# Attention stage of a fused transformer kernel: a unit's products in a new order, and the normalisation on GpSimd

## Chip and metric
One NeuronCore of one Trainium2 chip runs the program. The metric is the device time in microseconds (us) of one execution.

## Reference
Six sublayers, each fed by a layer norm, act on x of shape (8, 512, 128): expert FFN, RWKV attention, expert FFN, top-1 MoE, causal attention, top-1 MoE. The change touches the fifth:

```
x = x + 0.5 * _L1_ffn_ref(_layernorm(x))          # the stage before
# _L1_attn_ref(_layernorm(x)): 16 heads of d_k = 8, 512 tokens
qkv = einsum('bsm,qhkm->qbhsk', x, w_qkv); Q, K, V = qkv
scores = where(causal, einsum('bhsk,bhtk->bhst', Q, K) / sqrt(d_k), -inf)
attn = einsum('bhst,bhtk->bhsk', softmax(scores), V)
x = x + einsum('bsd,md->bsm', attn_cat, w_o)
x = x + 0.5 * _L1_ffn_ref(_layernorm(x))          # the stage after
```

## The kernel before
It is written engine by engine. Every engine runs its own program in order: TensorE (PE, matmuls), VectorE (DVE), ScalarE (ACT), GpSimd (POOL) and SyncE (SP, which only issues DMAs). Semaphores tie them together; a wait that is not yet met holds back all that stands behind it on its engine. x lies in SBUF throughout.

Attention works on 8 sequences b, each in NG = 4 units g of four heads: unit u = 4b + g, 32 units. Each head has 32 rows of the array (its high and low fp16 parts side by side), so that the score products of the four heads use the four row groups. A unit's key scores (keys down, queries across, only the causal part) are KT = 12 tiles t: tiles 0 to 3 (heads 0 to 3) hold 512 columns, 4 to 7 hold 384, 8 to 11 hold 256 + 128. by_key computes tile t into PSUM bank 4 + t % 2 and first waits until ACT's exps has emptied that bank, that is for the exp of tile t - 2. exps(u, g, t) (L938) writes the probabilities, POOL's mask (L620) zeroes the part above each diagonal, and weighted_values (L2036) multiplies by V in four column groups in fp32, for j = 0 to 3 (keys j*128 on), for the unit before. ACT copies that result (values, L950), PE transposes it (transpose_values, L2043), DVE divides by the sums (normalise, L1497, L1501).

The maximum that an exp subtracts enters through an extra row of the query stack. So two units ahead, by_query (L2019) computes the scores again with queries down, in QT = 6 groups n of two heads each, in banks 0 to 3; products of a bf16 identity and a mask (L2023) add the causal mask, 128 columns each; DVE's maxima (L1490) reduces. Then max_rows (L1995) transposes the maxima of a whole unit, ACT copies them (max_copy, L945), and SP loads them into the query stack (L458). by_key waits for that DMA (s_mmax) at t = 0.

Q, K and V of the next sequence are projected one each at fixed places of units g = 0 and 1 (q_proj, k_proj, v_proj; L1590 to L1592), each through PSUM bank 7, copied by ACT (q_high L925, k_high L931, v_copy L955), completed by DVE (q_low L1475, k_low L1479), and regrouped by head by SP's DMAs (stack, L451 for Q, L453 for K). transpose_out, out_proj (L2049 and L1590 to L1592), out_high, out_low and add finish the sequence before. x of a later sequence is normalised for the next stage by prep_bn, prep_aggr, prep_rstd, prep_norm (L1037), prep_transpose (L1580).

SP's program of the stage, after the start:

```
for u in range(UNITS - 1):
    max_rows(u + 1)                  # waits s_mTc, then the DMA that s_mmax counts
    if u % NG == 0 and u // NG < NB - 1:
        for g in range(NG):
            stack(u // NG + 1, g)    # wait s_mqlo, DMA Q; wait s_mklo, DMA K
```

PE's order in a unit: before tile t, the weighted values at t = 1, 3, 5, 5; tile t; with every even t a query group with its masks; max_rows after t = MAX_AT[g] = (2, 4, 2, 4); q_proj at t = 6 and k_proj at t = 10 of g = 0; v_proj at t = 8 of g = 1; transposes and output projections at t = 6, 8, 10 of g = 2 and 3. On ACT, k_high stands behind exp 11 of g = 0; on DVE, k_low stands behind the maxima n = 0 of g = 1. The loop over sequences is Fori over pairs for b = 1 to 4, the others are written out.

Of the kernel before, what the change touches and what calls it, by code (L numbers as in the profile page):

```python
# [14 lines left out]
P = 128  # L15
# [60 lines left out]
def build(nc, x, ffn_router, ffn_w, lin, col, bias, con, half, big, out):  # L76
    with ExitStack() as ctx:
# [130 lines left out]
        neg_max = [carve(HG * SUB) for _ in range(2)]  # L208
        max_row = carve(P, F16)
# [177 lines left out]
        s_p1, s_p1used = sem("scores_by_query_in_psum"), sem("scores_by_query_used")  # L387
# [89 lines left out]
        def _(pool):  # L477
# [9 lines left out]

            def clear_bias():
                pool.wait_ge(s_wlo, 3 * E)
                pool.memset(bias_raw, 0.0).then_inc(s_bz, 1)  # L490
# [48 lines left out]
            def moe(ph):  # L539
# [3 lines left out]
                def norm(bx):  # L543
                    n = n0 + SUB * bx
                    pool.wait_ge(s_rstd, n + SUB)
                    pool.wait_ge(s_xT, n)
                    for q in range(SUB):
                        ins = pool.tensor_scalar(x_norm[:, q * P:(q + 1) * P], sub(x_tok, SUB * (bx % NB) + q), ln_neg[:, q:q + 1],
                                                 ln_rstd[:, q:q + 1], ALU.add, ALU.mult)
                    ins.then_inc(s_xn, SUB)  # L550

# [17 lines left out]
                norm(2)  # L569
                for b in range(NB):  # L570
                    if b:
                        add(b - 1)
                    if b + 3 < last:
                        prep_rstd(n0 + SUB * (b + 3))
                        norm(b + 3)
# [34 lines left out]
            def attention(ph, start, rest):  # L610
# [32 lines left out]
        def _(act):  # L643
# [266 lines left out]
            def attention(ph, start, rest):  # L910
# [105 lines left out]
        def _(dve):  # L1016
# [453 lines left out]
            def attention(ph, start, rest):  # L1470
# [10 lines left out]
                def maxima(u, g, n):  # L1481

                    if n == 0 and not (isinstance(u, int) and u < 2):
                        dve.wait_ge(s_mTp, u - 1)
                    dve.wait_ge(s_p1, QT * u + n + 1)
                    r, pieces = query_tile(n)
# [36 lines left out]
                def body(b, odd, first, prep, more):  # L1523
# [3 lines left out]
                    for g in range(NG):  # L1527
                        u = NG * b + g
                        for n in range(QT):
                            if more or g < NG - 2:  # L1530
                                maxima(u + 2, (g + 2) % NG, n)
                            if n == 0 and g == 1 and more:
                                k_low(b + 1)
                            if n == 4 and g == 0 and more:
                                q_low(b + 1)
                            if n == 4 and g == 2 and not first:
                                out_low(b - 1)
                            if n == 0 and g == 3 and not first:
                                add(b - 1)
                            if n == 4 and not (first and g == 0):  # L1540
                                normalise(u - 1, b - (g == 0), (g - 1) % NG, odd ^ (g == 0))
                            if n == 2 and g == 1 and prep:
                                prep_bn(nx, SUB * bx)
                            if n == 3 and g == 1 and prep:
                                prep_aggr(nx)
                            if n in (1, 2) and g == 2 and prep:
                                prep_norm(nx, SUB * bx, range(2 * n - 2, 2 * n))
# [27 lines left out]
        def _(pe):  # L1575
# [394 lines left out]
            def attention(ph, start, rest):  # L1970
# [21 lines left out]
                def max_rows(u, g):  # L1992

                    pe.wait_ge(s_p1used, QT * (u + 1) + 2)
# [15 lines left out]
                def by_query(u, b, g, n, odd):  # L2010
                    first, pieces = query_tile(n)
# [4 lines left out]
                    for m, (i, at) in enumerate(pieces):  # L2016
                        for x in range(2):
                            rows = head(first + x)
                            pe.matmul(bank(2 * (n % 2) + x, at, at + (i + 1) * P), q_stack[odd][g][rows, i * P:(i + 1) * P], k_stack[odd][g][rows, 0:(i + 1) * P],  # L2019
                                      start=m == 0, stop=False, skip_group_check=True)  # L2020
                    for m, (i, at) in enumerate(pieces):
                        for x in range(2):
                            ins = pe.matmul(bank(2 * (n % 2) + x, at + i * P, at + (i + 1) * P), ident_b, keys_after,  # L2023
                                            start=False, stop=True, skip_group_check=True)
                    ins.then_inc(s_p1, 1)
# [44 lines left out]
                for u in range(2):  # L2070
                    for n in range(QT):
                        by_query(u, 0, u, n, 0)
                        keep_warm(1, 6)
# [154 lines left out]
```

## Time and profile before

| | us |
|---|---|
| median of 3 runs | 1806.04 |
| lowest, highest | 1795.75, 1809.79 |
| profiled execution, its own time | 1796.81 |
| its span, first to last instruction | 1794.7 |
| mean granted TensorE clock, share of full | 0.98 |

The profile records one execution. Its times are microseconds from the start of the span, and the views below are rows of it: engine busy times, groups of instructions by line, and timelines in which neighbouring instructions of one line are merged (x8 is eight of them, and the duration runs from the first's start to the last's end). A matmul's duration holds its latency, so back-to-back starts tell its cost. The bracket at the end of a row is idle time of that engine before it and what the profile takes to have ended it.

### The profile page before, as it was taken

What the parts mean: (1) busy time and instruction counts of PE and PEld (TensorE: products, weight loads), DVE (VectorE), ACT (ScalarE), POOL (GpSimd) and SP (SyncE); (2) the same over time, 40 slices, a digit from 0 to 9 for tenths busy, and PEclk for the clock granted to TensorE, in tenths of its full rate; (3) what the DMA queues carried; (4) which work ended last, traced back from release to release, by engine and by line L of the source; (5) the groups of instructions that cost most, each with busy time, mean ns of one, the idle gap of its engine ahead of it and who ended that gap; (6) DMA issues with size and microseconds to landing.
All of it is one profiled execution on the core that took longest, in us unless ns stands there. A gap on an engine that the chain in (4) does not pass through costs nothing. (4 is left out here: it accounts for less than half of the span.)

```text
span 1794.7 us, 45173 instructions
## 1 busy us (share of the span) xinstructions
PE 1691.7 (94%) x15966; PEld 1000.2 (56%) x15966; DVE 1226.7 (68%) x2848; ACT 1017.1 (57%) x1956; POOL 876.7 (49%) x722
## 2 busy tenths in 40 slices
PE   7899999999998999979999999999999998999988
PEld 4566666666665666646666666666644343434334
DVE  5865666666667888746665665666678786888566
ACT  5655555555555566545555555566533775777633
POOL 2665765665541435556755655765443222232232
PEclk9999999999999999999999999999999998999889
DMA  4200000000000000000000000000001110111000
GB/s 144 85 20 1 0 0 0 0 0 1 2 1 2 2 0 0 2 1 1 2 1 0 0 0 0 0 1 1 2 1 25 28 37 15 43 28 25 2 13 35
DMA packets 14617, 23.41 MB, mean 13 GB/s; under 512 B 2570, under 2 KB 10890, under 8 KB 14356
## 3 DMA queue, kind: packets, MB, share of 16 engines
q1 hardware_dynamic: 14484, 21.62, 4.2%
q8 instruction: 85, 1.39, 0.3%
q14 instruction: 48, 0.39, 0.1%
HBM read 11.00 MB, written 2.10 MB: 7 GB/s over the span
## 5 line engine op out<-in xcount | busy, mean ns | idle before, releaser
L506 POOL TENSOR_TENSOR scratch<-scratch 128x512 f16<-128x512 f32 x384 | 445.5, 1160 | 416.6 <-ACT scratch L667 416.3
L667 ACT ACTIVATE scratch<-scratch 128x512 f16<-128x512 f32 x512 | 322.4, 630 | 440.7 <-DVE scratch L1110 440.6
L1110 DVE SCALAR_TENSOR_TENSOR scratch<-psum,scratch 128x512 f32<-128x512 f32 x512 | 352.9, 690 | 313.8 <-ACT scratch L662 180.1
L1628 PE MATMUL psum<-ffn_down_hi,scratch 128*128 128x128 f16 x2048 | 369.3, 219 | 2.5 <-POOL scratch L506 2.1
L1630 PE MATMUL psum<-ffn_down_hi,scratch 128*128 128x128 f16 x2048 | 369.2, 219 | 0.0
L1629 PE MATMUL psum<-ffn_down_lo,scratch 128*128 128x128 f16 x2048 | 369.2, 219 | 0.0
L662 ACT ACTIVATE scratch<-psum 128x512 f32<-128x512 f32 x512 | 296.7, 580 | 0.0
L1490 DVE TENSOR_REDUCE scratch<-psum 128x2 f32<-128x1024 f32 (+3 forms) x256 | 202.4, 822 | 56.7 <-PE psum L2023 53.5
L1628 PEld LDWEIGHTS psum<-ffn_down_hi,scratch 128*128 128x128 f16 x2048 | 200.3, 98 | 60.4 <-POOL scratch L506 3.1
L1629 PEld LDWEIGHTS psum<-ffn_down_lo,scratch 128*128 128x128 f16 x2048 | 200.4, 98 | 56.1
L1590 PE MATMUL psum<-x_hi,ffn_up_hi 128*128 (+1 forms) x512 | 195.7, 382 | 7.8 <-DVE scratch L1110 7.6
L1630 PEld LDWEIGHTS psum<-ffn_down_hi,scratch 128*128 128x128 f16 x2048 | 200.4, 98 | 0.0
L1590 PE MATMUL psum<-x_hi,ffn_gate_hi 128*128 (+1 forms) x512 | 194.7, 380 | 3.6 <-ACT scratch L662 2.7
L1591 PE MATMUL psum<-x_lo,ffn_up_hi 128*128 (+1 forms) x512 | 195.1, 381 | 0.0
L1592 PE MATMUL psum<-x_hi,ffn_up_lo 128*128 (+1 forms) x512 | 195.0, 381 | 0.0
L1591 PE MATMUL psum<-x_lo,ffn_gate_hi 128*128 (+1 forms) x512 | 194.8, 380 | 0.0
L1592 PE MATMUL psum<-x_hi,ffn_gate_lo 128*128 (+1 forms) x512 | 194.7, 380 | 0.0
L499 POOL TENSOR_TENSOR scratch<-e_const,scratch 128x16 f32<-128x16 f32 x56 | 163.4, 2917 | 0.0
L480 POOL TENSOR_TENSOR ln_rstd<-ln_var,neg_half 128x4 f32<-128x4 f32 x48 | 48.5, 1010 | 210.8 <-DVE ln_var L1030 210.8
L1125 DVE SCALAR_TENSOR_TENSOR x_tok<-psum,scratch,x_tok 128x128 f32 (+1 forms) x512 | 143.2, 343 | 5.3 <-DVE scratch L1100 2.9
L938 ACT ACTIVATE scratch<-psum 128x384 f32<-128x384 f32 x256 | 116.3, 490 | 43.0 <-PE psum L2006 41.7
L1117 DVE TENSOR_TENSOR scratch<-scratch 128x512 f16<-128x512 f32 x128 | 88.8, 694 | 52.6 <-ACT scratch L667 50.1
(225 smaller groups left out, 2861.6 us busy)
## 6 DMA issues: line engine op xcount, KB each, us to landing
raw<-in_ffn_w_dram SPq DMA_DIRECT2D x8, 768.0 KB, 4.5
scratch<-scratch SPq DMA_DIRECT2D x32, 128.0 KB, 2.7
ffn_up_hi<-scratch SPq DMA_DIRECT2D x32, 128.0 KB, 2.7
x_tok<-in_x_dram SPq DMA_DIRECT2D x8, 256.0 KB, 6.7
out_dram<-x_tok SPq DMA_DIRECT2D x8, 256.0 KB, 2.0
raw<-in_lin_dram SPq DMA_DIRECT2D x1, 1092.0 KB
half_sb<-in_half_dram SPq DMA_DIRECT2D x1, 544.0 KB, 5.7
con_sb<-in_con_dram SPq DMA_DIRECT2D x1, 410.5 KB, 5.1
```

The costliest lines, as they stand in the source:

```text
L499: pool.tensor_tensor(lg_exp[:, c], e_const[:], lg_shift[:, c], ALU.pow).then_inc(s_exp, 1)
L506: pool.tensor_tensor(h_lo[r], h32[r], h_hi[r], ALU.subtract).then_inc(s_plo, 1)
L662: act.activation(gate_act[k % 2], bank(k % 2), ACT.Silu, scale=W_DOWN).then_inc(s_s, 1)
L667: act.activation(h_hi[k % HSLOTS], h32[k % HSLOTS], ACT.Copy).then_inc(s_hhi, 1)
L1110: dve.scalar_tensor_tensor(h32[k % HSLOTS], bank(5 + k % 2), W_DOWN, gate_act[k % 2], ALU.mult, ALU.mult).then_inc(s_h, 1)
L1490: ins = dve.tensor_reduce(neg_max[g % 2][:, a:a + SUB + 1:SUB], scores[:, :, at:at + (i + 1) * P], AX_X, ALU.max, negate=True)
L1590: pe.matmul(dst, lhs[0], rhs[0], start=first, stop=False)
L1591: pe.matmul(dst, lhs[0], rhs[1], start=False, stop=False)
L1592: return pe.matmul(dst, lhs[1], rhs[0], start=False, stop=last)
L1628: pe.matmul(dst, h_hi[r][:, cols], hi, start=k % FC == 0 and n == 0, stop=False, skip_group_check=True)
L1629: pe.matmul(dst, h_hi[r][:, cols], lo, start=False, stop=False, skip_group_check=True)
L1630: ins = pe.matmul(dst, h_lo[r][:, cols], hi, start=False, stop=k % FC == FC - 1 and n == SUB - 1, skip_group_check=True)
```

## The change
PE's unit gets a written-out order: five stretches of row-tiled key and query products, each followed by at most one lump of other products (masks, weighted values, a projection, transposes). Weighted values j = 0 move to the end of their own unit. The query groups n = 0 and 2 hold four diagonal blocks of two heads, whose masks are then one product of 512 columns per head; groups 1, 3, 4, 5 hold the blocks left of the diagonal without masks, and their maxima (neg_left) are joined to the diagonals' by a DVE min, which a new semaphore s_mneg reports. max_rows is placed after tile 2 in all units, the projections of Q, K, V and the output projection in the second stretch of g = 0, 1, 2, 3. ACT's and DVE's parts are moved to fit: k_high behind exp 7 of g = 1, k_low behind the maxima n = 3 of g = 1. The normalisation of x in this stage goes from DVE to POOL (prep_norm there). SP's program is unchanged. Its core (hunks shortened; each "..." marks what is left out):

```diff
-        MAX_AT = (2, 4, 2, 4)
...
-            return (2, 0)[n % 2], ([(3, 0)], [(2, 0), (0, 3 * P)], [(1, 0)])[n // 2]
+            return (2, 0, 0, 2, 0, 2)[n], (0, 1, 0, 1, 2, 2)[n]
+
+        LEFT = {1: [(3, 0), (1, 3 * P)], 2: [(2, 0)]}
...
@@ POOL, attention
-                            if g == 1 and j == 0 and prep:
+                            if g == 1 and j == 2 and prep:
                                 prep_rstd(n0 + SUB * b + LEAD)
+                            if g == 2 and j == 0 and prep:
+                                prep_norm(n0, b + 2)
@@ ACT, attention
-                            if t == MAX_AT[g] + 2 and (more or g < NG - 1):
+                            if t == 2 and (more or g < NG - 1):
                                 max_copy(u + 1, (b + (g + 1) // NG, (g + 1) % NG))
+                            if t == 5 and not (first and g == 0):
+                                values(u - 1)
+                            if t == 6 and g == 2 and more:
+                                v_copy(b + 1, 1 - odd)
                             if t == 7 and g == 0 and more:
                                 q_high(b + 1)
-                            if t == 11 and g == 0 and more:
+                            if t == 7 and g == 1 and more:
                                 k_high(b + 1)
-                            if t == 6 and not (first and g == 0):
-                                values(u - 1)
-                            if t == 9 and g == 1 and more:
-                                v_copy(b + 1, 1 - odd)
-                            if t == 7 and g == 2 and not first:
+                            if t == 9 and g == 2 and not first:
                                 out_high(b - 1)
@@ DVE, maxima
-                    for i, at in pieces:
-                        a = r * SUB + i
-                        ins = dve.tensor_reduce(neg_max[g % 2][:, a:a + SUB + 1:SUB], scores[:, :, at:at + (i + 1) * P], AX_X, ALU.max, negate=True)
+                    if kind == 0:
+                        ins = dve.tensor_reduce(neg_max[g % 2][:, r * SUB:(r + 2) * SUB], by(psum[:, 2 * (n % 2) * BANK:2 * (n % 2 + 1) * BANK], 2 * SUB),
+                                                AX_X, ALU.max, negate=True)
+                    else:
+                        for i, at in LEFT[kind]:
+                            a = r * SUB + i
+                            ins = dve.tensor_reduce(neg_left[g % 2][:, a:a + SUB + 1:SUB], scores[:, :, at:at + i * P], AX_X, ALU.max, negate=True)
                     ins.then_inc(s_p1used, 1)
+                    if n == QT - 1:
+                        dve.wait_ge(s_p1used, QT * u + QT + 2)
+                        whole, left = [by(t, HG)[:, :, 1:SUB] for t in (neg_max[g % 2], neg_left[g % 2])]
+                        dve.tensor_tensor(whole, whole, left, ALU.min).then_inc(s_mneg, 1)
@@ DVE, attention
-                            if n == 0 and g == 1 and more:
+                            if n == 2 and not (first and g == 0):
+                                normalise(u - 1, b - (g == 0), (g - 1) % NG, odd ^ (g == 0))
+                            if n == 3 and g == 0 and more:
+                                q_low(b + 1)
+                            if n == 3 and g == 1 and more:
                                 k_low(b + 1)
-                            if n == 4 and g == 0 and more:
-                                q_low(b + 1)
...
@@ PE, attention
-                    pe.wait_ge(s_p1used, QT * (u + 1) + 2)
+                    pe.wait_ge(s_mneg, u + 1)
                     pe.transpose(bank(7, 0, P)[0:HG * SUB], neg_max[g % 2], ident).then_inc(s_mTp, 1)
...
+                    if kind == 0:
+                        for i in range(SUB):
+                            for x in range(2):
+                                rows, block = head(first + x), slice(i * P, (i + 1) * P)
+                                pe.matmul(bank(2 * (n % 2) + x)[:, block], q_stack[odd][g][rows, block], k_stack[odd][g][rows, block],
+                                          start=i == 0, stop=False, skip_group_check=True)
+                    else:
+                        for i, at in LEFT[kind]:
...
+                def mask_later(n):
+
+                    if query_tile(n)[1] == 0:
                         for x in range(2):
+                            ins = pe.matmul(by(bank(2 * (n % 2) + x), SUB), ident_b, keys_after.rearrange("p (o k) -> p o k", o=1).to_broadcast([P, SUB, P]),
                                             start=False, stop=True, skip_group_check=True)
...
+                        keys(0, 1)
+                        queries(0)
+                        keys(2)
+                        mask(0)
+                        if turns:
...
+                            if g == 1 and more:
+                                pe.wait_ge(s_mqlo, b + 2)
+                            if g == 2 and more:
+                                pe.wait_ge(s_mklo, b + 2)
...
+                            max_rows(u + 1, (g + 1) % NG)
+                        if follows:
+                            weighted_values(*before, 1)
+
+                        keys(3, 4)
+                        queries(1)
+                        if follows:
+                            weighted_values(*before, 2)
+                            weighted_values(*before, 3)
+                        if g == 0 and more:
+                            turned()
+                            q_proj(b + 1)
+                        if g == 1 and more:
+                            turned()
+                            k_proj(b + 1)
+                        if g == 2 and more:
+                            turned()
+                            v_proj(b + 1)
+                        if g == 3 and not first:
+                            turned()
+                            out_proj(b - 1)
+
+                        keys(5, 6)
+                        queries(2)
+                        mask(2)
+                        if follows:
+                            transpose_values(u - 1)
+
+                        keys(7, 8)
+                        queries(3)
+                        keys(9)
...
+                            transpose_out(b - 1, 1 - odd)
+                        if g == 3 and prep:
...
+                            prep_transpose(n0 + SUB * b + LEAD, 7)
+
+                        keys(10)
+                        queries(4)
+                        keys(11)
+                        queries(5)
+                        weighted_values(u, b, g, odd, 0)
...
-                for j in range(SUB):
+                for j in range(1, SUB):
                     weighted_values(UNITS - 1, NB - 1, NG - 1, 1, j)
```

## Rows read from the trace of the kernel before

**Rows 1.** The page, busy us of each engine.

```profile
PE 1691.7 (94%) x15966; PEld 1000.2 (56%) x15966; DVE 1226.7 (68%) x2848; ACT 1017.1 (57%) x1956; POOL 876.7 (49%) x722
```

**Rows 2.** Timeline, PE: tile 0 of units 4, 6, 8, 10, 12, 14.

```profile
1424.64 0.39 PE L2006 MATMUL psum<-ffn_up_hi 32*128 32x512 f16 x1 [0.54 <-ACT scratch L938]
...
1444.75 0.39 PE L2006 MATMUL psum<-ffn_up_hi 32*128 32x512 f16 x1 [0.54 <-ACT scratch L938]
...
1463.69 0.39 PE L2006 MATMUL psum<-scratch 32*128 32x512 f16 x1 [0.54 <-ACT scratch L938]
...
1484.17 0.38 PE L2006 MATMUL psum<-scratch 32*128 32x512 f16 x1 [0.87 <-ACT scratch L938]
...
1510.62 0.60 PE L2006 MATMUL psum<-ffn_up_hi 32*128 32x512 f16 x1 [3.57 <-issue]
...
1532.79 0.39 PE L2006 MATMUL psum<-ffn_up_hi 32*128 32x512 f16 x1 [0.54 <-ACT scratch L938]
```

**Rows 3.** Windows: stretch, length, each engine's busy us (instructions), granted clock, DMA, GB/s.

```profile
1428.50:1468.00 39.50, 36.33 (x388) 16.42 (x390) 32.26 (x58) 28.50 (x63) 10.94 (x17) 1.00 0.13 29
...
1485.00:1490.00 5.00, 5.00 (x28) 0.79 (x28) 2.81 (x4) 1.36 (x3) 0.52 (x1) 0.50 0.00 0
...
1510.00:1515.00 5.00, 4.38 (x20) 0.89 (x20) 1.25 (x2) 1.37 (x3) 0.00 (x0) 0.50 0.01 3
```

**Rows 4.** Timeline, ACT: exps of 512 and 384 columns, values, k_high.

```profile
1435.28 1.02 ACT L931 ACTIVATE scratch<-psum 128x1024 f16<-128x1024 f32 x1
...
1447.01 1.08 ACT L938 ACTIVATE ffn_gate_hi<-psum 128x512 f32<-128x512 f32 x2 [1.15 <-PE psum L2006]
...
1451.01 0.60 ACT L950 ACTIVATE scratch<-psum 128x512 f32<-128x512 f32 x1
...
1452.37 1.42 ACT L938 ACTIVATE scratch<-psum 128x384 f32<-128x384 f32 x3
```

**Rows 5.** Timeline, PE: a projection, then a stretch of unit 6.

```profile
1430.39 0.38 PE L1590 MATMUL psum<-x_hi,scratch 128*128 x1
1430.61 0.38 PE L1591 MATMUL psum<-x_lo,scratch 128*128 x1
...
1446.59 0.39 PE L2006 MATMUL psum<-ffn_up_hi 32*128 32x512 f16 x2
1446.59 0.59 PE L2019 MATMUL psum<-scratch 32*128 32x512 f16 x2
1447.12 0.29 PE L2023 MATMUL psum<-big_sb 128*128 128x128 bf16 x2
1447.24 0.27 PE L1995 MATMUL psum<-con_sb,scratch 128*16 128x128 f32 x1
1447.44 0.85 PE L2036 MATMUL psum<-scratch,ffn_down_lo 128*32 128x384 f32 x8
1448.23 0.38 PE L2006 MATMUL psum<-ffn_up_hi 32*128 32x512 f16 x2
```

**Rows 6.** Timeline, PE: tile 10 of unit 6.

```profile
1452.92 0.28 PE L2006 MATMUL psum<-ffn_up_hi 32*128 32x256 f16 x1 [0.34 <-ACT scratch L938]
```

**Rows 7.** Timelines, DVE's k_low and SP's DMA issues in unit 5.

```profile
1436.46 0.68 DVE L1479 SCALAR_TENSOR_TENSOR scratch<-psum,scratch 128x512 f16<-128x512 f32 x1
...
1437.17 0.59 SPq L453 DMA_DIRECT2D scratch<-scratch  x1
...
1441.71 8.66 SPq L458 DMA_DIRECT2D ffn_up_hi<-scratch  x2
```

**Rows 8.** Timelines, SP and ACT ahead of unit 10.

```profile
1478.81 1.36 SPq L453 DMA_DIRECT2D ffn_up_hi<-scratch  x1
...
1481.92 0.59 SPq L458 DMA_DIRECT2D scratch<-scratch  x1
...
1483.29 0.88 ACT L938 ACTIVATE scratch<-psum 128x384 f32<-128x384 f32 x2
```

**Rows 9.** Groups by line: DVE's and POOL's normalisation, busy us, mean ns.

```profile
L1037 DVE TENSOR_SCALAR x_norm<-x_tok,ln_mv,ln_rstd 128x128 f32 (+1 forms) x24 | 7.1, 340 | 0.0
...
L548 POOL TENSOR_SCALAR x_norm<-x_tok,scratch,ln_rstd 128x128 f32<-128x128 f32 x32 | 13.9, 448 | 0.8
```

More of the change, by code:

```diff
@@ L208, in build @@
         neg_max = [carve(HG * SUB) for _ in range(2)]
+        neg_left = [carve(HG * SUB) for _ in range(2)]
         max_row = carve(P, F16)
@@ L486, in _, with prep_norm @@
             pool.wait_ge(s_pool_const, 2)
+            def prep_norm(n0, bx):
+                n = n0 + SUB * bx
+                pool.wait_ge(s_rstd, n + SUB)
+                pool.wait_ge(s_xT, n)
+                for q in range(SUB):
+                    ins = pool.tensor_scalar(x_norm[:, q * P:(q + 1) * P], sub(x_tok, SUB * (bx % NB) + q), ln_neg[:, q:q + 1],
+                                             ln_rstd[:, q:q + 1], ALU.add, ALU.mult)
+                ins.then_inc(s_xn, SUB)
             def clear_bias():
@@ L541, in moe @@
                 t0 = use * NS
[L543 to L550, printed above, removed]
                 def add(b):
@@ L2010, in by_query @@
                 def by_query(u, b, g, n, odd):
-                    first, pieces = query_tile(n)
+                    first, kind = query_tile(n)
                     if n == 0:
@@ L2015, in by_query @@
                     pe.wait_ge(s_p1used, QT * u + n + 1)
-                    for m, (i, at) in enumerate(pieces):
-                        for x in range(2):
[L2018 to L2023, printed above, removed]
+                    if kind == 0:
[6 more added lines that the diff above has]
+                        for i, at in LEFT[kind]:
+                            for x in range(2):
+                                rows = head(first + x)
+                                ins = pe.matmul(bank(2 * (n % 2) + x, at, at + i * P), q_stack[odd][g][rows, i * P:(i + 1) * P], k_stack[odd][g][rows, 0:i * P],
+                                                start=True, stop=True)
+                        ins.then_inc(s_p1, 1)
+                def mask_later(n):
+                    if query_tile(n)[1] == 0:
+                        for x in range(2):
+                            ins = pe.matmul(by(bank(2 * (n % 2) + x), SUB), ident_b, keys_after.rearrange("p (o k) -> p o k", o=1).to_broadcast([P, SUB, P]),
                                             start=False, stop=True, skip_group_check=True)
-                    ins.then_inc(s_p1, 1)
+                        ins.then_inc(s_p1, 1)
                 def weighted_values(u, b, g, odd, j):
@@ new lines, in body, with keys, queries, mask @@
+                        turns = more or g < NG - 1
+                        def keys(*tiles):
+                            for t in tiles:
+                                by_key(u, b, g, t, odd)
+                        def queries(n):
+                            if more or g < NG - 2:
+                                by_query(u + 2, b + (g + 2) // NG, (g + 2) % NG, n, odd ^ (g >= NG - 2))
+                        def mask(n):
+                            if more or g < NG - 2:
+                                mask_later(n)
@@ new lines, in turned @@
+                        def turned():
+                            if turns:
+                                pe.wait_ge(s_mTc, u + 2)
+                        keys(0, 1)
+                        queries(0)
+                        keys(2)
+                        mask(0)
+                        if turns:
+                            if g == 0 and first:
+                                pe.wait_ge(s_mv_in, 1)
+                            if g == 0 and not first:
+                                pe.wait_ge(s_xlo, n0 + SUB * b + LEAD)
+                            if g == 1 and more:
+                                pe.wait_ge(s_mqlo, b + 2)
+                            if g == 2 and more:
+                                pe.wait_ge(s_mklo, b + 2)
+                            if g == 3 and first:
+                                pe.wait_ge(s_mv_in, b + 2)
+                            if g == 3 and not first:
+                                pe.wait_ge(s_yolo, b)
+                            if g in (1, 2) and not more:
+                                pe.wait_ge(s_mTc, u + 1)
+                            max_rows(u + 1, (g + 1) % NG)
@@ new lines, in body @@
+                        if g == 2 and more:
+                            turned()
+                            v_proj(b + 1)
+                        if g == 3 and not first:
+                            turned()
[7 more added lines that the diff above has]
+                        queries(3)
@@ new lines, in body @@
+                        keys(9)
+                        if g == 2 and not first:
+                            if more:
+                                pe.wait_ge(s_mv_in, b + 2)
+                            else:
+                                turned()
+                            transpose_out(b - 1, 1 - odd)
+                        if g == 3 and prep:
+                            if first:
+                                turned()
+                            else:
+                                pe.wait_ge(s_mout, b)
+                            prep_transpose(n0 + SUB * b + LEAD, 7)
```

69 lines of the change are left out of this document (12 added, 57 removed).

## Prediction

> **What bounds the kernel now.** The page's busy line comes first [rows 1]: TensorE (PE) is busy 94% of the span, the next engine 68%. So a gain must shorten PE's path, and a loss needs only one thing that PE waits for. The change touches the attention stage alone. PE's timeline puts that stage's 32 units (one for 4 heads of one sequence) between 1387 and 1711 us. Four full-clock units, from the first key tile of unit 4 to that of unit 8, take 1463.69 - 1424.64 = 39.05 us, 9.76 us each [rows 2]. By engine this stretch holds 36.3 us of PE in 39.5, 32.3 of VectorE (DVE), 28.5 of ScalarE (ACT) [rows 3]. PE is the bound there, but ACT is close behind in one respect: key scores have two PSUM banks (4 and 5), so tile t cannot start before the exp of tile t-2 has ended. The reader should see in [rows 4] that an exp of 512 columns starts 0.42 us after its matmul (1446.59 in [rows 5] to 1447.01) and that two of them take 1.08, so 0.60 each with a start every 0.48 (for 384 columns 0.49 and 0.38, as the 0.88 of two ahead of unit 10 shows, below), and in [rows 6] that PE stood 0.34 us before 1452.92, until 0.06 after the end of the exp that began at 1452.37.
>
> The queue view comes last and matters most. SyncE (SP) issues its DMAs in program order. In unit 5 (g = 1) the first K stack goes out at 1437.17, and the maxima rows for unit 6 only behind all of them, at 1441.71 [rows 7]. Unit 6 began at 1444.75 [rows 2], so their landing took 3.04 us or less. Ahead of unit 10 one issue of the same series took 1.36 us, the maxima rows went out at 1481.92, and ACT's last two exps began at 1483.29 (the first of them, all that tile 0 needs, ended by 1483.78), yet PE's tile 0 started only at 1484.17 [rows 2, 8]. I find nothing else that was open, so I read the landing as 2.25 us after the issue began, and the chain as one that ends within a microsecond of its deadline already.
>
> **The stretches, part by part.** PE changes between three modes: row-tiled scores, full array (masks, projections, transposes), column-tiled weighted values. In [rows 5] two key and two query products start at 1446.59; two products of the busiest row group stream 2 x 0.213 = 0.43 us (512 columns each, as the 0.22 between the projection's matmuls shows); the mask starts at 1447.12, so the change of mode costs 0.10. Old unit: 15 such changes; new unit: 3, 2 or 3, 2, 0 or 2 and 2 in its five stretches, about 10. Saved: 5 x 0.105 = 0.5 us. Row groups also collide less: the streams of the busiest group sum to 2.13 us in the old six stretches (0.37, 0.43, 0.43, 0.37, 0.27, 0.27) and 1.81 in the new ones: 0.3 saved. The 16 masks of 128 columns (0.12 for two) become 4 of 512 (0.213): 0.05 saved. Total 0.85 us per unit, if nothing waits.
>
> The Trainium skill (TensorEngine Tiling (Array Packing), Key Properties) says that changing the tiling mode drains TensorE, and the 0.10 above agrees. The same page (Performance Considerations) warns that tiling speeds TensorE and not the emptying of PSUM. By the first rule alone the sum would be 31 x 0.5 = 16 us below the time of before; by the second it would be no gain at all, since PE then waits for exps, and the trace shows such waits already [rows 6].
>
> Walk of a new unit from its key tile 0 at 0. Tiles 0 and 1 and query group 0 start together; tile 2 needs the exp of tile 0: 0.42 + 0.60 + 0.06 = 1.08, and PE has nothing in between, since the mask stands behind tile 2 in the order. Mask at 1.40 (0.213 + 0.105), two masks 0.43, transpose of the maxima 0.28, weighted values 1 with the mode change behind them 0.75 (0.79 in [rows 5]): 2.86. Second stretch: tiles 3, 4, query 1 0.49, values 2 and 3 0.75, a projection 0.76: ends 4.86. Third: tiles 5, 6, query 2 0.49, masks 0.43: 5.8. The transposes of the values need ACT's copy (0.60 at 1451.01), which it issues behind exp 5: 4.86 + 0.37 + 0.38 + 0.59 + 0.06 = 6.26; with their 0.54 they end at 6.80. Fourth: tile 9 needs exp 7, which starts at 7.16: 7.71. Then a transpose group 0.54 in g = 2 and 3, or, in g = 0 and 1, the copy of Q or K (1.02 at 1435.28, 0.9 until the next can start) ahead of exp 8, which holds tile 10 until 9.0. Tiles 10 and 11, queries 4 and 5 and the values 0 (0.97) end the unit at 10.2 (g = 2, 3) and 10.7 (g = 0, 1). Four units: 41.8. The same walk over the old order gives 38.4 where the trace has 39.05, so the difference, 3.4 us per four units, is what I use: 8 x 3.4 = 27 us. The two waits of 0.7 and 0.45 us and the copy ahead of exp 8 thus eat the 0.85 and more. Bounds: a loss of 10 us, if half of these waits are filled by work whose ends I model too late; 47, if each of the 28 small query products costs as much issue time as a full 128-column one (0.056).
>
> **The queue.** The K projection moves from unit g = 0 into the second stretch of g = 1, ACT's copy behind exp 7 of g = 1, and DVE's low part from n = 0 to n = 3 of g = 1, behind the maxima of query group 3, a product of the fourth stretch. SP's program is not edited. It still has, behind the maxima rows of unit g = 1, the eight stack DMAs, seven of them behind the K low part, and then the maxima rows of unit g = 2, for which PE waits at tile 0. Priced: query 3 starts at 6.9 after the start of unit g = 1; its two reductions follow those of group 2 and a normalisation and end at 8.8, and ACT's K copy (from 7.54, behind exp 7) ends at 8.55; the low part (0.68 [rows 7]) ends at 9.5. The old one ended at 1437.14, 7.6 us before unit 6 began; the new one ends 1.2 before unit g = 2 would. Seven issues from 1437.17 to 1441.71 are 4.54 us: 14.05. Landing 2.25: 16.3. Unit g = 1 ends at 10.7. PE stands 5.65 us; queued behind its wait is everything PE has, so ACT and DVE run dry too. This happens for sequences 0 to 6: 7 x 5.65 = 40 us. Bounds: 36 (if DVE is 0.5 sooner) to 45 (landing 3.04).
>
> **The clock.** After the idle 3.57 us at 1510.62 (a loop's back edge) the granted clock is 0.50 from 1510 to 1515, that is 1.2 GHz [rows 2, 3]; this pair of units took 1532.79 - 1510.62 = 22.17 us, against 20.11 for units 4 and 5: +2.1. After a wait of 0.87 us before 1484.17 it was 0.50 from 1485 to 1490 too; that pair took 1510.62 - 1484.17 = 26.45, less 3.0 of loop idle 23.4, against 18.94 (units 6 and 7): +4.5. Each stall of 5.65 us should bring such an episode: 7 x 3.3 = 23, less the 4.5 of unit 10, which is in the old time: 19. Bounds: 10 (7 x 2.1 - 4.5) and 60, as the new order's own short waits may bring about nine more episodes of 4.5.
>
> **DVE, GpSimd, the rest.** The reductions keep their sizes: 2 of 1024, 2 of 768, 2 of 256, 2 of 512 per unit, two of them now as eight blocks, so none changes its price. Added: one min of 12 elements, whose own time is not in the trace; it lies between nothing and the 0.34 of the much larger normalisation [rows 9], I take 0.2 with its wait for DVE's last reduction; it is needed only by the next unit's transpose at 1.8, and PE's values 0 hide it. Without that cover it would cost 0.2 x 31 = 6 us. Removed from DVE: four normalisations of 0.34 per sequence; GpSimd does them at 0.45 in g = 2, behind mask 0 and ahead of mask 1; it is busy 10.9 us of 39.5 [rows 3], and PE transposes them only in g = 3: nothing on the path. DVE has 1.8 us free per unit [rows 3], so both are zero. Moving the values 0 one place earlier shifts 1 us and adds none.
>
> Sum against the profiled execution (1796.8 us, span 1794.7): 27 + 40 + 19 = 86, so 1883. The median of the runs shown is 1806.04, 9.2 above that execution, so 1892 on it.
>
> **Rivals.** (A) The clock does not recover between the waits. If ten more units lose what unit 10's pair lost, 10 x 4.5 = 45 and a little more come on top: about 1945. For it: the drop near 1485 needed little idling. Against: units 4 to 9 idle 0.8 each at clock 1.00. Chance 12%. (B) The maxima rows are not late, because the chain is shorter than I read it (the landing is not what held unit 10, or DVE gets to the low part sooner): only the unit loss stays, 27 us, 1833. DVE's low part would have to end 3.85 after the start of g = 1, when the K projection has not begun. Chance 6%. (C) Faster: the chain in time as in B, and PE's waits for exps filled, so that the 0.85 us per unit are kept: 31 x 0.85 = 26 us, 1780. It decides at PE's idle time before tiles 2, 9 and 10: below 0.8 us a unit it wins. Against it stand the issue order, and the walk's 1.08 for tile 2. Chance 3%. The edit that turns out as a relabelling (masks and groups at old cost, order harmless) would be 1806, 1%.
>
> **Numbers.** Forecast 78%, A 12%, B 6%, C 3%, no effect 1%. The range takes the bounds: 10 + 36 + 10 = 56 at the low end (1862), widened part way towards B to 1850; 47 + 45 + 60 = 152 would be the high end with every bound at once, 1958; I stop at 1940, which leaves out about half of A. Within 1% (18 us, about what a measurement of this kernel can tell from no change) and beyond it: B's near edge gives the middle some chance; faster 0.03, same 0.03, slower 0.94.
>
> **What would show it.** In the changed profile: SP issues the first K stack some 9.5 us into unit g = 1, the maxima rows 4.5 later; PE idles 5 to 6 us before the first key tile of each unit g = 2, seven times, with a granted clock of 0.5 behind it; pairs of other units at full clock take 20.4 to 21.4 us, with idle time before tile 2 and tile 10 released by ACT; DVE and ACT are not busier. I would be wrong if those seven gaps are missing, if full-clock units run below 9.7 us, or if the clock stays at half for most of the stage.

## The result, and the profile after

The changed kernel takes 1894.52 us, median of 4 runs (1890.14 to 1902.58), where the kernel before took 1804.03 on the same chip (median of 4): ratio 1.051, 95% interval 1.0453 to 1.0567. The forecast was 1892. The profiled execution is the slowest of the four, 1902.58 us (span 1900.7), 106 above that of before; the medians are 90.5 apart.

The page of the kernel after, busy us of each engine and the granted TensorE clock in 40 slices:

```profile
PE 1731.4 (91%) x15966; PEld 1006.5 (53%) x15966; DVE 1227.8 (65%) x2856; ACT 1025.1 (54%) x1956; POOL 890.5 (47%) x754
...
PEclk9999999999999999999999999999988878887679
```

Against [rows 1] PE executes as many instructions, but it is now busy 40 us longer, 34 of them in the attention stage (the last quarter of the row), where the clock digits are under 9: part of the work ran at half clock. The waits of PE in the stage (1380 to 1820 us): us in total, times, longest.

```profile
PE psum L2017 <- ACT scratch L942: 25.9, 49, 1.0
PE psum L2017 <- DMA scratch<-scratch: 21.8, 4, 5.9
PE psum L2017 <- DMA ffn_up_hi<-scratch: 16.8, 3, 6.4
PE psum L2065 <- ACT scratch L954: 11.4, 31, 1.1
```

Rows two and three are new: seven waits of a key tile (L2017) for a DMA, 38.6 us. PE's timeline at the longest, in sequence 1, with the unit g = 1 ahead of it:

```profile
1451.09 0.61 PE L2017 MATMUL psum<-ffn_up_hi 32*128 32x512 f16 x2
...
1461.46 0.33 PE L2017 MATMUL psum<-ffn_up_hi 32*128 32x256 f16 x2 [0.36 <-ACT scratch L942]
1462.76 0.28 PE L2017 MATMUL psum<-ffn_up_hi 32*128 32x256 f16 x1 [0.96 <-ACT scratch L942]
...
1470.99 0.71 PE L2017 MATMUL psum<-ffn_up_hi 32*128 32x512 f16 x2 [6.40 <-DMA ffn_up_hi<-scratch]
1472.36 0.60 PE L2017 MATMUL psum<-ffn_up_hi 32*128 32x512 f16 x1 [0.32 <-ACT ffn_gate_hi L942]
```

What DVE and SP did meanwhile (two timelines):

```profile
1462.58 0.68 DVE L1483 SCALAR_TENSOR_TENSOR scratch<-psum,scratch 128x512 f16<-128x512 f32 x1
```

```profile
1449.64 0.60 SPq L453 DMA_DIRECT2D scratch<-scratch  x1
1463.29 0.59 SPq L455 DMA_DIRECT2D scratch<-scratch  x1
1463.98 1.36 SPq L453 DMA_DIRECT2D scratch<-scratch  x1
...
1467.99 0.61 SPq L455 DMA_DIRECT2D scratch<-scratch  x1
1468.65 0.57 SPq L460 DMA_DIRECT2D ffn_up_hi<-scratch  x1
```

This is the chain, link by link: the low part of K (L1483) ends at 1463.26; the first K stack (L455) leaves 0.03 later, SP having waited for it since the first Q stack at 1449.64; seven issues take 5.36 us; the maxima rows (L460) leave last and PE starts 2.34 us after that. In [rows 7] the same series ran while PE still had work.

Inside a unit, the full-clock unit 4 (g = 0) from its tile 0:

```profile
1440.04 0.39 PE L2017 MATMUL psum<-ffn_up_hi 32*128 32x512 f16 x2
...
1441.20 0.39 PE L2017 MATMUL psum<-ffn_up_hi 32*128 32x512 f16 x1 [0.55 <-ACT ffn_gate_hi L942]
...
1446.38 0.66 PE L2065 MATMUL psum<-con_sb,scratch 128*128 128x128 f32 x4 [0.31 <-ACT scratch L954]
...
1447.88 0.33 PE L2017 MATMUL psum<-ffn_up_hi 32*128 32x256 f16 x2 [0.36 <-ACT scratch L942]
1449.18 0.28 PE L2017 MATMUL psum<-ffn_up_hi 32*128 32x256 f16 x1 [0.96 <-ACT scratch L942]
...
1449.97 1.18 PE L2058 MATMUL psum<-ffn_gate_hi,ffn_down_lo 128*32 128x512 f32 x8
```

The reader should see four idle stretches, each released by ACT: before tile 2 (an exp), before the transposes (the copy L954), before tiles 9 and 10 (exps). They are 2.2 us together. Windows in the same columns as [rows 3], of this unit, of the start of unit g = 1, and behind the long wait:

```profile
1440.00:1450.00 10.00, 7.79 (x88) 3.28 (x85) 7.71 (x13) 6.90 (x15) 2.49 (x4) 1.00 0.01 3
1451.00:1456.00 5.00, 4.24 (x31) 1.14 (x28) 2.14 (x6) 1.95 (x4) 0.77 (x2) 0.50 0.12 24
1471.00:1478.10 7.10, 6.78 (x47) 2.27 (x48) 2.52 (x3) 2.93 (x6) 1.22 (x3) 0.50 0.01 2
```

**Where the time went.** I measure units from one start of the product of 512 columns (values 0, L2058 here, L2036 before) to the next. In the profiled executions the first and the last of the 32 are 1710.45 - 1395.92 = 314.5 us apart before and 1813.25 - 1398.61 = 414.6 after: 100.1 of the 106. Of these, 38.6 are the waits for the maxima rows. At full clock four units took 39.05 before; after, a full-clock unit takes 10.9 in g = 0 and 1 and 10.26 in g = 3. No unit g = 2 ran at full clock throughout here; in e2 below, where they do, they take 10.26 too, from tile 0 to the next tile 0. Four units make 42.3, so 3.25 more, times 31/4: 25. The rest, 36.5, is what I put down to half clock: the granted clock between the two starts is 0.95 before and 0.79 after. Between the medians, 15 closer, it would be some 21 if the other parts are equal, which no run shows.

### The profile page after: what moved, and what is told of

The parts are those of the page before. It is cut to its first block and busy times, and to the rows that moved or that the text cites. A ratio compares the mean times of both kernels' runs of the same rounds, so it can differ in the third digit from the quotient of the medians.

```text
span 1900.7 us, 45246 instructions
## 1 busy us (share of the span) xinstructions
PE 1731.4 (91%) x15966; PEld 1006.5 (53%) x15966; DVE 1227.8 (65%) x2856; ACT 1025.1 (54%) x1956; POOL 890.5 (47%) x754
## 5 line engine op out<-in xcount | busy, mean ns | idle before, releaser
L671 ACT ACTIVATE scratch<-scratch 128x512 f16<-128x512 f32 x512 | 322.3, 630 | 440.5 <-DVE scratch L1114 440.4
L1494 DVE TENSOR_REDUCE scratch<-psum 128x8 f32<-128x1024 f32 x64 | 78.3, 1224 | 134.4 <-PE psum L2045 125.2
L622 POOL TENSOR_SCALAR_AFFINE_SELECT scratch<-scratch 128x512 f32<-128x512 f32 x96 | 59.8, 634 | 159.5 <-ACT scratch L942 159.5
```

The source lines that it names most:

```text
L671: act.activation(h_hi[k % HSLOTS], h32[k % HSLOTS], ACT.Copy).then_inc(s_hhi, 1)
```

## The experiments

Each was compared with the kernel before on its own chip; e9 and e10 ran on another chip than the rest, so they are set beside the others by their ratios. Where "units" are given, they are the distances just defined, in the profiled execution.

**e1: the queue alone.** SP sends the Q stacks behind the maxima rows for unit g = 1 as before, but the K stacks only behind those for unit g = 2, so the rows that unit g = 2 waits for no longer stand behind K's low part.

```diff
-                    if u % NG == 0 and u // NG < NB - 1:
+                    if u % NG < 2 and u // NG < NB - 1:
...
-                            stack(u // NG + 1, g)
+                            (q_stacked, k_stacked)[u % NG](u // NG + 1, g)
```

> The changed kernel with SP's program alone altered: behind the maxima rows of unit g = 0 stand only the four Q stacks, and the four K stacks follow the maxima rows of unit g = 2. The queue theory: the seven gaps of 5.4 us before tile 0 of units g = 2 go; query group 0 of those units then waits for the first K stack, issued about 9.6 us into unit g = 1 and landed 2.7 later, 1 to 2 us. That gives back 7 x 4 = 28 us and some of the clock episodes behind the gaps, 10 to 20 more: 1845 to 1865 beside 1895. If the order of the products or the clock by itself made the loss, the time stays above 1885.

Measured 1865.4, ratio 1.0364 (1.0346 to 1.0381): 29 less than after and 0.4 above the range expected. PE's timeline at the same place, then SP's:

```profile
1470.76 0.61 PE L2034 MATMUL psum<-scratch 32*128 32x128 f16 x8 [2.33 <-DMA scratch<-scratch]
```

```profile
1466.59 3.69 SPq L457 DMA_DIRECT2D scratch<-scratch  x4
1473.29 0.58 SPq L462 DMA_DIRECT2D ffn_up_hi<-scratch  x1
```

No key tile waits for the maxima rows any more. The K stacks are as late as they were, so the first query group (L2034) of the seven units g = 2 waits for them instead: four waits that the profile puts down to the DMA, 4.6 us, and three, 2.2 us, that it puts down to issue, at the same place of the unit and each ending 2.7 us after the first K stack left. That the stalls come from the order of the queue is shown; their 38.6 less 6.8 would be 32, and 29 came back on the medians.

The 10 to 20 us of clock episodes that were to go with the stalls did not come on top. The units g = 2 still take 12.9 to 14.0 us, 86.2 in sum without their waits, against 92.1 in the kernel after without theirs and about 71 at full clock. The stall did not make the clock fall. Windows of the kernel after (its stall there is 5.28 us, before tile 0 at 1634.25), then of e1, where tile 0 starts at 1616.11 with no wait before it:

```profile
1626.00:1628.30 2.30, 1.42 (x16) 0.56 (x16) 2.30 (x5) 2.07 (x5) 0.63 (x2) 1.00 0.01 4
1628.30:1629.00 0.70, 0.67 (x4) 0.00 (x0) 0.56 (x2) 0.00 (x0) 0.70 (x2) 0.50 0.34 51
```

```profile
1612.00:1614.60 2.60, 1.29 (x14) 0.67 (x18) 2.54 (x5) 2.56 (x6) 0.64 (x1) 1.00 0.01 3
1614.60:1616.11 1.51, 1.51 (x9) 0.01 (x2) 1.03 (x3) 0.28 (x1) 1.10 (x2) 0.50 0.35 66
```

PE is at work when the clock falls, and what both have ahead of it are the short waits of unit g = 1, 0.36 and 0.96 us. In the kernel after the seven falls lie between 1.5 us before the start of a stall and 0.6 after it.

**e2: does the idle time cost clock?** 88 small products fill PE's long wait; nothing they write is used.

```diff
+                        if g == 2 and more:
+                            pe.wait_ge(s_p2exp, KT * u + 1)
+                            keep_warm(22, 4)
                         keys(0, 1)
```

> The changed kernel with 88 matmuls of an identity (their product is overwritten) placed in the idle gap before tile 0 of units g = 2, once the exp of tile 10 has emptied bank 4. They take 4.9 us at full clock, so the gap's length stays and only its emptiness goes. The clock theory: no half-clock episode behind the gap, 7 x 2 to 3 us less: 1875 to 1882. If the clock falls whatever PE does there, no change, 1895.

Measured 1892.4, ratio 1.0512 (1.0487 to 1.0537): 2 less than after, so the number missed. The timeline:

```profile
1472.18 6.61 PE L1597 MATMUL psum<-half_sb 128*128 128x128 f16 x88
1478.72 0.39 PE L2017 MATMUL psum<-ffn_up_hi 32*128 32x512 f16 x2
1479.88 0.39 PE L2017 MATMUL psum<-ffn_up_hi 32*128 32x512 f16 x1 [0.76 <-ACT ffn_gate_hi L942]
```

The unit behind the fill does run at full clock (key tiles 0.39, not the 0.71 above), and the seven units g = 2 with their waits are 16.5 to 18.0 long instead of 17.5 to 19.5, which is 119.2 in sum instead of 130.7, 1.6 each. From first to last unit it is 400.8 us against 414.6. But the median doesn't follow, and the half clock in units g = 1 (13.5) is untouched. The clock had fallen before the fill and came back during it, which is why the fill took 6.61 us and not the 4.9 forecast:

```profile
1472.00:1475.40 3.40, 3.40 (x35) 3.22 (x32) 0.36 (x2) 0.00 (x0) 1.96 (x3) 0.50 0.79 179
1475.40:1478.70 3.30, 3.30 (x60) 3.22 (x58) 0.00 (x0) 0.00 (x0) 0.00 (x0) 1.00 0.42 100
```

At this place the fill also ran some 0.4 us beyond the wait, if the maxima rows, issued at 1475.93, needed the 2.34 of above. So the emptiness of the wait decides whether the clock is still down behind it; that it fell was not the wait's doing, as e1 shows. What this is worth over a whole run the experiment doesn't settle.

**e3: something for PE to do ahead of tile 2.** Mask 0 and the transpose of the maxima now stand before tile 2 instead of behind it.

```diff
-                        keys(2)
                         mask(0)
...
                             max_rows(u + 1, (g + 1) % NG)
+                        keys(2)
```

> The changed kernel with mask 0 and the transpose of the maxima ahead of key tile 2 instead of behind it. The walk: PE's wait for exp 0 (0.67 us idle) is filled with 0.7 us of full-array work, at one more change of mode (0.1): 0.4 to 0.55 us per unit, 13 to 17 us in all, and with fewer half-clock episodes up to 25: 1870 to 1882. The rival, that mode changes are what costs, gives 0.1 x 32 = 3 us more: 1898.

Measured 1881.0, ratio 1.0449 (1.0419 to 1.0479): 13.5 less than after, in number as expected. In the timeline of a unit g = 3 the wait before tile 2 is gone:

```profile
1483.74 0.39 PE L2017 MATMUL psum<-ffn_up_hi 32*128 32x512 f16 x2
1483.75 0.40 PE L2031 MATMUL psum<-scratch 32*128 32x128 f16 x8
1484.08 0.60 PE L2045 MATMUL psum<-big_sb 128*128 128x512 bf16 x2
1484.80 0.27 PE L2006 MATMUL psum<-con_sb,scratch 128*16 128x128 f32 x1
1485.00 0.39 PE L2017 MATMUL psum<-ffn_up_hi 32*128 32x512 f16 x1
```

The parts are not the walk's, which gave every unit 0.4 to 0.55 us. At full clock the units g = 0 are 0.1 shorter and the units g = 3 0.3; the only full-clock unit g = 1 is 0.6 shorter. The half-clock units g = 1 take 11.8 to 12.8 instead of 13.5 to 13.7, so a part of the 13.5 is clock. How much, no run separates.

**e4: the diagonal groups alone.** The kernel before with the new query groups, each mask behind its group, and the min.

> The kernel before with the diagonal groups alone (query groups, masks of 512 columns, DVE's min, s_mneg), in the old order of products. By the row-tile and mode prices: three groups a unit lose their masks and with them one or two mode changes each where no full-array work stands beside them, 0.2 to 0.4 us per unit where PE is the bound: 6 to 12 us faster than before, 1792 to 1798. If the eight small products cost issue time, or the min delays the maxima, 0 to 5 us slower: 1804 to 1809.

Measured 1821.74, ratio 1.0144 (1.0108 to 1.018): 22 us slower than before and outside both ranges expected. One stretch of its timeline, and the row of the kernel before that ends the stretch which answers to it, begun at 1448.23 in [rows 5]:

```profile
1434.35 0.38 PE L2018 MATMUL psum<-ffn_up_hi 32*128 32x512 f16 x2
1434.47 0.46 PE L2032 MATMUL psum<-ffn_up_hi 32*128 32x128 f16 x8
1434.87 0.60 PE L2046 MATMUL psum<-big_sb 128*128 128x512 bf16 x2
1435.40 0.86 PE L2059 MATMUL psum<-scratch,ffn_down_hi 128*32 128x256 f32 x16
1436.19 0.34 PE L2018 MATMUL psum<-ffn_up_hi 32*128 32x384 f16 x2
```

```profile
1449.88 0.33 PE L2006 MATMUL psum<-ffn_up_hi 32*128 32x384 f16 x2
```

The diagonal groups put all the masks of a pair of heads into one stretch: it takes 1.84 us here and 1.65 before. The stretches without a mask get shorter, but there PE waits for exps: in a unit with no half clock the key tiles wait 0.36, 0.47 and 0.54 us for ACT (1555.81, 1558.51, 1559.38), where before they wait 0.26 and 0.54. The three units there take 10.54, 9.67 and 10.67 (the last of them ends at half clock, its key tile at 1559.38 taking 0.60), where the same three of before take 10.37, 9.33 and 9.52. The first two alone give 0.25 a unit, 8 us over the stage; all three, with their bit of half clock, 0.55 and 17. What part of the 22 is half clock and what the new lumps, no run separates.

**e5: the old query groups in the new order.** The kernel after with the groups, masks (each behind its group, mask 0 and mask 2 where they are in after) and reductions of before.

> The changed kernel with the old query groups and their 16 masks of 128 columns, in the new order of products (mask 0 and mask 2 where they were, the others right behind their group). If the diagonal groups are bad by themselves, as their 22 us in the old order suggest, this gives some of it back: 1873 to 1885 beside 1895. If their cost in the old order was one of place only (two lumps of 0.43 us where PE is the bound, and savings where it waits for ACT), the masks of groups 1, 4 and 5, now 0.3 us each with their changes of mode, come on top: 0.3 to 0.6 us per unit, 1904 to 1914.

Measured 1901.59, ratio 1.0562 (1.0514 to 1.0611), between the two ranges expected and nearer the second. The units at full clock are 10.68 and 11.10 where after has 10.26 and 10.92, which is 0.3 a unit or 9 us over the stage; the intervals of the two kernels' ratios overlap, so that the groups help in the new order rests on the unit lengths and only weakly on the times.

**e6: the normalisation alone.** The kernel before with x normalised on GpSimd.

> The kernel before with the normalisation of x on GpSimd alone. Off every path, so no change: 1797 to 1804 beside 1800. If DVE's 1.4 us per sequence counted, 3 to 8 us faster; if GpSimd's 1.8 us ahead of mask 1 delayed the weighted values, 3 to 10 slower.

Measured 1798.28 against 1801.24, ratio 0.9991 (0.9974 to 1.0008): nothing, as priced.

**e7: e1 and e3 together.**

> SP's order of e1 and the mask-first order of e3 together in the changed kernel. They mend different waits, so both gains add: 1895 - 29 - 13.5 = 1852 (1846 to 1858). If the clock episodes overlap (one mend makes the other's episodes vanish too) up to 10 lower; if the shorter unit only makes the K stack later for group 0, up to 10 higher.

Measured 1841.19, ratio 1.022 (1.0192 to 1.0248): 53 less than after, where the two gave 29 and 13.5 alone, and 1 below the lowest time expected. The surplus of 11 is clock, I suppose, since the granted clock between the first and the last unit is 0.87 here and 0.79 in after; no run separates it. In PE's timeline the waits before tiles 9 and 10 are those of after, and so is the one for the copy:

```profile
1632.03 0.66 PE L2068 MATMUL psum<-con_sb,scratch 128*128 128x128 f32 x4 [0.31 <-ACT scratch L957]
1633.53 0.33 PE L2020 MATMUL psum<-ffn_up_hi 32*128 32x256 f16 x2 [0.36 <-ACT scratch L945]
1634.83 0.28 PE L2020 MATMUL psum<-ffn_up_hi 32*128 32x256 f16 x1 [0.96 <-ACT scratch L945]
```

**e8: the copies fitted to the order too.** e7, and ACT copies the values' product behind exp 4 (not 5) and Q's or K's high part behind exp 4 (not 7), DVE makes the low parts after query group 1 (not 3).

```diff
-                            if t == 5 and not (first and g == 0):
+                            if t == 4 and not (first and g == 0):
...
-                            if t == 7 and g == 0 and more:
+                            if t == 4 and g == 0 and more:
...
-                            if n == 3 and g == 0 and more:
+                            if n == 1 and g == 0 and more:
```

> e7 and ACT's copy of the weighted values behind exp 4 instead of 5, its Q and K copies behind exp 4 instead of 7, DVE's low parts behind the maxima n = 1 instead of 3. The walk: the wait before the transposes of the values (0.31), the 0.96 before tile 10 of g = 0 and 1 and the wait for the first K stack go; four full-clock units come to 38.2 to 39.5 us beside 39.05 of the kernel before: 1795 to 1812 in all. If the queue was not all of it, or the clock stays down in spite of the filled waits, 1815 to 1840.

Measured 1817.44, ratio 1.0094 (1.0068 to 1.0119): 5 above the expected range, so the number missed. The waits for the copies are nearly gone, but a new one stands before the last query group, for DVE: 0.47 us in the units g = 2 and 3, 1.00 and 1.07 in g = 0 and 1, 21 us in all.

```profile
1618.16 0.39 PE L2040 MATMUL psum<-ffn_up_hi 32*128 32x256 f16 x2 [1.00 <-DVE scratch L1502]
1618.48 1.93 PE L2061 MATMUL psum<-ffn_gate_hi,ffn_down_lo 128*32 128x512 f32 x8
...
1629.68 0.28 PE L2040 MATMUL psum<-ffn_up_hi 32*128 32x256 f16 x2 [1.07 <-DVE scratch L1502]
```

**e9 and e10: which early step makes that wait.** e9 takes back one step of e8, Q's low part, to query group 3; e10 also puts K's low part one group later.

> The kernel of e8_all_mended with one of its moves taken back: the fp16 remainder of the queries (q_low) is again the DVE step at query group 3, as in the kernel after, the one of the keys stays at group 1. In the profile of e8 the last query group of the units g=0 and g=1 waits 1.00 and 1.07 us for the reduction L1502 (1618.16, 1629.68), where it waits 0.47 in the units g=2 and g=3; DVE does q_low (0.69 us) in the unit g=0 ahead of three reductions. Theory: DVE's order makes that wait, so in units g=0 it falls by some 0.6 us, and with it may go the half clock behind it (the values' product at 1618.48 took 1.93 instead of 1.06). 7 x 0.6 = 4 us, up to 7 x 1.8 = 13 us with the clock: 1804 to 1814 after e8's 1817. Rival: the query stacks leave later and the first query group waits for them, as in e7: no gain or 2 to 5 us more, 1817 to 1822.

> As e9_late_q_low, and the keys' remainder (k_low) one query group later as well (behind the second pair of maxima instead of the first). Theory of DVE's order: the last wait of the unit g=1 (1.07) falls little, since k_low still stands ahead of the reduction it waits for: within 3 us of e9. Rival: key stacks leave 1.2 us later, in e8 they left at 1626.77 and are wanted at 1630.89 after four issues and a landing of 2.3 us, so the first query group of the unit g=2 waits: 4 to 10 us more than e9.

Measured 1810.13, ratio 1.0057 (1.0039 to 1.0075), and 1813.27, ratio 1.0059 (1.0024 to 1.0093). The interval of e9 just touches that of e8, so that e9 is faster rests on the timeline more than on the times. In e9 the wait of g = 0 is down to 0.37, that of g = 1 stays:

```profile
1604.73 0.28 PE L2040 MATMUL psum<-ffn_up_hi 32*128 32x256 f16 x2 [0.37 <-DVE scratch L1502]
...
1616.33 0.39 PE L2040 MATMUL psum<-ffn_up_hi 32*128 32x256 f16 x2 [1.07 <-DVE scratch L1502]
```

DVE's order makes the wait of g = 0, as the theory says; that of g = 1 is still 1.03 in e10, as it says too. e10's rival (a wait for the key stacks) didn't come: only one query group waits for a DMA in it, 0.3 us. In e9 four full-clock units take 1667.52 - 1628.68 = 38.84, the 39.05 of before within 0.2. Its first and last unit are 322.3 apart, 7.8 more than before, and since its full-clock units are no longer and the loop's back edge is not either (2.87 us against 3.57), that is half clock: 0.905 between the two starts against 0.945. No version with the new order beats the kernel before. A fill for the short waits, to test the clock by itself, was not tried.

## Why the prediction was right, point by point

**The queue, 40 us (36 to 45): right.** Seven gaps before the first key tile of the units g = 2, 38.6 us in sum, and e1 shows their cause. Its links: seven issues in 5.36 us at the place shown (4.54 forecast, one of them again taking 1.36), landing and start 2.34 (2.25 forecast from one indirect place). The low part of K ended later than the forecast 9.5 us into unit g = 1 (12.2 at the place shown), because that unit ran at half clock for part of its way; it delayed the end of the unit as well, so the gap is not far longer. (By its own terms the gap is 5.6, not 5.65, and rival B's deadline 3.9, not 3.85; neither changes the sum.)

**The unit, 27 us: right in the sum and nearly in the parts.** 3.25 us per four units against 3.4, so 25. (The walk is some 0.5 short for the new order and 0.65 for the old, and only the difference was used.) Tile 2 at 1.16 after tile 0 in unit 4 and 1.07 in unit 3 (forecast 1.08), the transposes at 6.34 (6.26), tile 9 at 7.84 (7.71), tile 10 at 9.14 (9.0); the unit is 10.26 in g = 3, and in g = 2 of e2 (10.2), and 10.9 in g = 0, 1 (10.7). e3 shows the first wait to be a matter of order, and e8 and e9 the other three: with nearly all taken away the new order's four units are as long as the old ones, no shorter.

**The 0.85 us a unit of work saved: not confirmed as a gain of the groups.** I priced the fewer row-group collisions and masks as a saving that waits eat. In the new order e5 puts the groups at 0.3 a unit, in the right direction. In the old order e4 makes them a loss, 0.25 a unit in the two units that are free of half clock and 22 us in all. The step of mine that fails there is that a shorter sum of products is worth something or nothing: it matters too how the products are spread over stretches that are bound by PE and by ACT.

**The clock, 19 us (10 to 60): right in size on the medians (some 21), 36 in the profiled execution, and wrong in its mechanism.** I had each stall bring an episode of its own, 3.3 us. The half clock was there: behind each long wait the unit g = 2 took 10.98 to 12.47 from its tile 0 to its values 0, where 9.2 is the full-clock length (8.4 in the first sequence), 2.8 each and some 20 in all. But e1 has no such wait, and some 15 of the 21 us by which the units g = 2 of the kernel after exceed full clock are still there in it (86.2 and 92.1 against about 71). The clock falls behind the short waits of unit g = 1; the stall only adds to it. The rest came from where I had foreseen no definite episode: 6 of the 7 units g = 1 with a projection took 13.5 to 13.7 instead of 10.9, behind the short waits of unit g = 0, and the last three units ran at half clock throughout. I had given such episodes only to the upper bound, 4.5 each; those of g = 1 cost 2.65. That the total comes within 3 us of the forecast is therefore luck in this term: the episodes cost less than I priced, and there were more of them. That the short waits cause them is argued from their place, and from e8, where PE idles 1.07 us in a unit g = 1 instead of 2.4 and four of the seven units g = 2 run at full clock (9.5 to 9.6); no run tests it alone.

**The normalisation, 0: right** (e6). **DVE and GpSimd, 0: right for the change as made**; e8 shows how little room it had, as DVE does bound the end of a unit as soon as PE's waits for ACT are gone.

**The rivals.** A (the clock stays down, 1945) is out: windows of full clock stand between the episodes (1.00 from 1440 to 1450), and the median is 50 below it. B and C are out, since the maxima rows were late and the waits for exps stayed.

## What to carry to other kernels

When an order of products is changed, walk the in-order queues of the other engines too: SP's program was not edited, and the move of one projection by one unit put seven DMAs behind a late operand and a needed one behind them; sending the needed one first gave 29 us. Removing the stalls did not bring the clock back, since short waits ahead of them had lowered it (e1). Before pulling work together into lumps, look for the two banks whose release paces PE, and keep something to do between a tile and the one two further on. In e4 fewer streamed columns made a slower kernel: the stretches without masks waited for ACT, and the one with the masks got longer.

## What the runs showed of the hardware that was not expected

The clock fell to half after idle times that are short and spread out: in unit 4 waits of 0.36 and 0.96 us within 2 us, with PE busy 7.79 of the 10 us around them, were followed by 5 us at 0.50 (1451 to 1456 in the windows above). The same waits stand before unit g = 1 of sequence 4 (0.36 at 1614.65, 0.96 at 1615.95), and there the kernel after stayed at full clock (window):

```profile
1617.00:1622.00 5.00, 4.24 (x53) 1.40 (x46) 2.97 (x9) 3.07 (x7) 1.43 (x3) 1.00 0.12 26
```

That unit took 10.89 us. So such waits make an episode likely and not certain. The clock was at 0.50 from 1450.8 to 1457.6 behind these short waits, and for 7.1 us behind the idle 6.4 us, about as long. A unit g = 1 with 6.8 us at half clock is 2.65 us longer, and not the 3.4 that half of them would be. I suppose that the slower products fill part of its waits for ACT.
